# The last block of a fused attention and expert feed-forward kernel: z products by halves, one rounding remainder on GpSimd, another order on VectorE

## The reference, cut to what matters

```python
t = nx.reshape(-1, Dq)
probs = softmax(t @ gate_w.T); topw, topi = top_k(probs, 2); topw /= sum(topw)
h1 = t @ w1.T + 2.0 * (t @ a1[e].T) @ b1[e].T
h3 = t @ w3.T + 2.0 * (t @ a3[e].T) @ b3[e].T
act = silu(h1) * h3                                   # 512 wide, per expert
out_e = act @ w2.T + 2.0 * (act @ a2[e].T) @ b2[e].T  # 128 wide
out = sum_e weights[e] * out_e
x = x + out
```

## Time and profile before

| | us |
|---|---|
| median of three runs | 297.6 |
| span of the profiled execution | 296.7 |
| PE busy | 287.4 (97%) |
| DVE busy | 221.4 (75%) |
| ACT busy | 187.5 (63%) |
| POOL busy | 187.0 (63%) |

### The profile page before, as it was taken

How to read it: one execution, slowest core, us unless ns; L and a number is a source line. 1 busy time by engine, 2 the same in 40 slices (tenths; PEclk the granted TensorE clock), 3 DMA queues, 4 the chain that set the end, 5 groups by cost and what they waited for, 6 DMA issues and landing times. The chain is left out here.

```text
span 296.7 us, 4518 instructions
## 1 busy us (share of the span) xinstructions
PE 287.4 (97%) x1487; PEld 238.4 (80%) x1487; DVE 221.4 (75%) x607; ACT 187.5 (63%) x310; POOL 187.0 (63%) x186
## 2 busy tenths in 40 slices
PE   8779999999999999999999999999999999999995
PEld 6557888878888888888888888888888887878874
DVE  3878986995689658894589765895579965795295
ACT  1467967674945966757755868459656658655532
POOL 3375599288970889419990589608982389518930
PEclk9979999999999999999999999999999999999999
DMA  5720020200220021200211011200012000200002
GB/s 147 287 66 9 0 73 1 72 1 11 97 73 0 0 72 38 71 1 2 71 50 60 0 49 59 71 0 2 1 37 73 0 0 35 75 1 0 0 2 71
DMA packets 7225, 12.45 MB, mean 42 GB/s; under 512 B 1825, under 2 KB 3234, under 8 KB 7202
## 3 DMA queue, kind: packets, MB, share of 16 engines
q1 hardware_dynamic: 6768, 11.77, 12.0%
q10 hardware_dynamic: 434, 0.39, 0.4%
HBM read 10.03 MB, written 2.13 MB: 41 GB/s over the span
## 5 line engine op out<-in xcount | busy, mean ns | idle before, releaser
L989 ACT ACTIVATE silu<-h_ps 128x512 f32<-128x512 f32 x64 | 37.4, 596 | 31.4 <-PE h_ps L641 29.8
L1639 POOL TENSOR_TENSOR um_lo<-umf,um_hi 128x1024 fp32r<-128x1024 f32 x7 | 16.9, 2414 | 60.5 <-ACT um_hi L981 60.5
L641 PE MATMUL h_ps<-um_hi,b_hi 128*128 128x512 f32 x128 | 51.4, 401 | 0.0
L641 PE MATMUL h_ps<-um_lo,b_hi 128*128 128x512 f32 x128 | 50.3, 393 | 0.5 <-DVE um_lo L1309 0.5
L641 PE MATMUL h_ps<-um_hi,b_lo 128*128 128x512 f32 x128 | 49.9, 390 | 0.0
L1322 DVE TENSOR_TENSOR act_first<-silu,h_ps 128x512 f32<-128x512 f32 x32 | 21.4, 680 | 20.9 <-ACT silu L989 16.1
L1322 DVE TENSOR_TENSOR act_second<-silu,h_ps 128x512 f32<-128x512 f32 x32 | 21.7, 679 | 16.6 <-PE h_ps L641 14.7
L1661 POOL TENSOR_TENSOR scaled<-act_second,ratio 128x512 f32<-128x512 f32 x24 | 31.5, 1313 | 1.3 <-DVE act_second L1322 1.3
L641 PEld LDWEIGHTS h_ps<-um_lo,b_hi 128*128 128x128 f32 x128 | 24.0, 188 | 6.9 <-DVE um_lo L1309 1.4
L981 ACT CAST um_hi<-umf 128x1024 fp32r<-128x1024 f32 x14 | 14.8, 1055 | 23.2 <-DVE umf L1303 22.2
L641 PEld LDWEIGHTS h_ps<-um_hi,b_lo 128*128 128x128 f32 x128 | 24.1, 188 | 4.5
(11 more groups left out here) (278 smaller groups left out, 789.2 us busy)
## 6 DMA issues: line engine op xcount, KB each, us to landing
chosen<-choice_dram SPq DMA_DIRECT2D x7, 512.0 KB, 3.6
x_in<-in_x_dram SPq DMA_DIRECT2D x7, 256.0 KB, 2.9
ctx_in<-in_ctx_t_dram SPq DMA_DIRECT2D x7, 256.0 KB, 3.2
out_dram<-y SPq DMA_DIRECT2D x7, 256.0 KB, 2.0
act_second<-in_hidden_w_dram SPq DMA_DIRECT2D x1, 512.0 KB, 4.1
act_second<-in_lora_w_dram SPq DMA_DIRECT2D x1, 512.0 KB, 5.6
v_parts<-in_down_w_dram SPq DMA_DIRECT2D x1, 512.0 KB, 5.3
ctx_in<-in_ctx_t_dram ACTq DMA_DIRECT2D x2, 128.0 KB, 3.2
```

The lines of the kernel that those rows point to most:

```text
L641: mm = nc.tensor.matmul((h1_ps, h3_ps)[s][n % 2][:], b13[w][:, s, c * P:(c + 1) * P], um[k][m][:, s, :], start=False, stop=(i == 2), skip_ ...
L989: nc.scalar.activation(silu[:, n % SILU_RING, :], h1_ps[n % 2][:], ACT.Silu).then_inc(silu_done.sem, 1)
L1639: nc.gpsimd.tensor_tensor(um[1][1][:], umf[1][:], as_f32(um[1][0][:]), ALU.subtract)\
```

## The change: what it does

In the last block alone:

- `z_ps` is split by halves of two tiles: half 0 in `z_ps`, half 1 in `h3_ps[1]`, a bank that the hidden steps have left free; each half has its own completion count (`last_a2z_mm`). A 512-column matmul becomes two of 256 columns, all three terms of half 0 before those of half 1.
- the w2 products of the two halves, so far alternating, come apart: half 0 of all chunks first, then half 1, with `last_b2(0)` ahead of the last product of half 1.
- the lo part of chunk 3 of b moves from DVE to POOL (`last_b_low`), as POOL's last instruction.
- DVE does both `total`s and then both `z_low`s, then both halves of the b part of v, then `finish(LAST - 1)`, and then part, sum and lo part half by half.

```diff
-LAST_W2_ORDER = (1, 0, 3, 2)
+LAST_W2_FIRST = 1
+        last_z = (z_ps, h3_ps[1])
@@ a2_product
+                elif b == LAST and (c, k) == (3, 1):
+                    pe.wait_ge(last_b_lo, 1)
+                if b == LAST and k == 0:
+                    if c == first:
+                        pe.wait_ge(act_done.sem, act_done.of(LAST))
+                    for h in range(2):
+                        for i, (w, m) in enumerate(TERMS):
+                            mm = nc.tensor.matmul(last_z[h][:, 0:HALF], w2a2[w][:, c, D:D + ER],
+                                                  split[m][:, c, half(h)], start=(c == first and i == 0),
+                                                  stop=(c == last and i == 2), skip_group_check=True)
+                        if c == last:
+                            mm.then_inc(last_a2z_mm, 1)
+                    return
@@ PE, order of the last block
             a2_product(LAST, 0, 1)
-            w2_product(LAST, 1)
+            last_w2(1, 0)
             a2_product(LAST, 2, 1)
             a2_product(LAST, 0, 0)
+            a2_product(LAST, 1, 0)
             a2_product(LAST, 3, 1)
-            a2_product(LAST, 1, 0)
             a2_product(LAST, 2, 0)
             a2_product(LAST, 3, 0)
-            w2_product(LAST, 0)
-            w2_product(LAST, 3)
-            w2_product(LAST, 2)
+            last_w2(0, 0)
+            last_w2(2, 0)
+            last_w2(3, 0)
+            last_w2(1, 1)
+            last_w2(0, 1)
+            last_w2(2, 1)
             last_b2(0)
+            last_w2(3, 1)
             last_b2(1)
@@ POOL
+            def last_b_low():
+                pool.wait_ge(b_hi_done.sem, b_hi_done.of(LAST, 3))
+                nc.gpsimd.tensor_tensor(b_split[1][:, PARTS[2], :], act_second[:, PARTS[2], :],
+                                        as_f32(b_split[0][:, PARTS[2], :]), ALU.subtract).then_inc(last_b_lo, 1)
...
             scale_step(LAST, 2)
+            last_b_low()
```

More of the change, by code:

```diff
@@ L240, in build_program @@
         y_bank, out_bank = even_ps, odd_ps
-        last_out, last_turned = (odd_ps, h1_ps[0]), (even_ps, h3_ps[0])
+        last_out, last_turned, last_z = (odd_ps, h1_ps[0]), (even_ps, h3_ps[0]), (z_ps, h3_ps[1])
         choice_dram = nc.dram_tensor("choice_dram", (2, P * CHOICE), F32).ap()
@@ L361, in build_program @@
         stored = signal("stored", 16)
+        last_b_lo = sem("last_b_lo")
+        last_a2z_mm = sem("last_a2z_mm")
         last_v_part = [sem("last_v_part0"), sem("last_v_part1")]
@@ L691, in w2_product @@
                     pe.wait_ge(z_lo_done.sem, z_lo_done.of(b, c - 1))
-                first = (FIRST_W2_ORDER if b == 0 else LAST_W2_ORDER if b == LAST else W2_ORDER)[0]
+                first = (FIRST_W2_ORDER if b == 0 else W2_ORDER)[0]
                 if c == first:
-                    if b + 1 < BLOCKS:
-                        pe.wait_ge(t_hi_done.sem, t_hi_done.of(b + 1))
-                        pe.wait_ge(t_lo_done.sem, t_lo_done.of(b + 1))
-                    else:
-                        pe.wait_ge(o_t_done.sem, o_t_done.of(b - 1))
-                        pe.wait_ge(silu_done.sem, silu_done.of(b))
-                        pe.wait_ge(act_done.sem, act_done.of(b))
+                    pe.wait_ge(t_hi_done.sem, t_hi_done.of(b + 1))
+                    pe.wait_ge(t_lo_done.sem, t_lo_done.of(b + 1))
@@ new lines, in w2_product, with last_w2 @@
+                for i, (w, m) in enumerate(TERMS):
+                    nc.tensor.matmul(out_bank[:], w2a2[w][:, c, 0:D], z_split[m][:, c, :],
+                                     start=(c == first and i == 0), stop=False, skip_group_check=True)
+            def last_w2(c, h):
+                if c < 2:
+                    pe.wait_ge(z_lo_pair.sem, z_lo_pair.of(LAST))
+                else:
+                    pe.wait_ge(z_lo_done.sem, z_lo_done.of(LAST, c - 1))
+                if c == LAST_W2_FIRST:
+                    if h == 0:
+                        pe.wait_ge(o_t_done.sem, o_t_done.of(LAST - 1))
+                    else:
+                        pe.wait_ge(silu_done.sem, silu_done.of(LAST))
+                        pe.wait_ge(act_done.sem, act_done.of(LAST))
@@ L701, in w2_product @@
                 for i, (w, m) in enumerate(TERMS):
[L702 to L708, removed]
+                    nc.tensor.matmul(last_out[h][:, 0:HALF], w2a2[w][:, c, 0:D], z_split[m][:, c, half(h)],
+                                     start=(c == LAST_W2_FIRST and i == 0), stop=False, skip_group_check=True)
@@ L1390, in last_part @@
             def last_part(k, i):
-                done = (a2z_mm, a2b_mm)[k]
-                ve.wait_ge(done.sem, done.of(LAST))
                 if k == 1:
+                    ve.wait_ge(a2b_mm.sem, a2b_mm.of(LAST))
                     ve.wait_ge(mask_scaled.sem, mask_scaled.of(LAST))
+                else:
+                    ve.wait_ge(last_a2z_mm, i + 1)
                 ve.wait_ge(v_done.sem, v_done.of(LAST - 1))
-                nc.vector.scalar_tensor_tensor(out=v_parts[:, k, half(i)], in0=(z_ps, b_ps)[k][:, half(i)],
+                src = last_z[i][:, 0:HALF] if k == 0 else b_ps[:, half(i)]
+                nc.vector.scalar_tensor_tensor(out=v_parts[:, k, half(i)], in0=src,
                                                scalar=LORA_SCALE, in1=masks[LAST % 2][:, k, half(i)],
@@ L1558, in _ @@
             total(LAST, 2)
-            b_low(LAST, 2)
             total(LAST, 3)
             z_low(LAST, 1)
+            z_low(LAST, 2)
             last_part(1, 0)
-            z_low(LAST, 2)
+            last_part(1, 1)
             finish(LAST - 1)
             last_part(0, 0)
+            last_sum(0)
             last_part(0, 1)
-            last_sum(0)
-            last_part(1, 1)
+            last_low(0)
             last_sum(1)
-            last_low(0)
             last_low(1)
```

## The result

The changed kernel takes 299.79 us (median of 10 runs, 298.72 to 300.02) against 298.38 for the kernel before in the same comparison (10 runs). The ratio is 1.0045, 95% interval 1.003 to 1.0059: 1.3 us slower by the ratio (the medians lie 1.41 apart), inside the forecast's "no change, near its edge". The profiled execution has a span of 298.2 against 296.7. Two executions, one of e9 (736.43) and one of the kernel before (891.33), took more than twice the usual time and are left out of every ratio.

What follows compares the result with a forecast made beforehand. The prediction took PE and DVE as full in the last block, DVE having to come free earlier too. +1.10 - 0.60 + 0.34 + 0.18 = +1.02, plus 0.25, is +1.27: span about 298.0, time 298.9 us, range 297.4 to 299.9.

Steps and rivals of the forecast that it cites:

- no change, near its edge: Whole kernel: forecast 0.4% slower, within the about 0.5% (1.5 us) that a measurement can't tell from no change; chance 0.73.
- Two engines full, both late at once: Last block, 284.5 to 288.0: PE and DVE busy 3.50 of 3.50 us, ending together at 289.29 and 289.31.
- POOL's b_lo blocks DVE's total, +1.10: Last block: POOL's b_lo gets in behind DVE's scaled, so DVE's first total ends at 286.63, +1.10 us.
- the starved case: Rival: DVE keeps winning, POOL's b_lo ends only at 288.69 and PE waits; 300.0 us, 0.8% slower; chance 0.12.
- the shared one: Rival: beside POOL each two-operand DVE instruction takes 0.3 longer, two totals +0.60; 298.4 us; chance 0.10.
- no blocking: Rival: POOL's b_lo and DVE's totals don't block each other in any way worth naming; 297.8 us; chance 0.15.
- -0.60, +0.34, +0.18 to the z part: DVE ahead of v's z part: one b_lo less -0.60, second b part moved ahead +0.34, ACT waits +0.18.
- New order of v, +0.25: Last block, from v's z part to the second b2 product: 3.24 us in place of 2.99, +0.25.
- The halves hidden: PE's z in halves: half 0 done 0.36 us before half 1, but the gain is hidden behind DVE.
- The sum, +1.27: Whole kernel: +1.02 to the z part and +0.25 behind it, span 296.7 to about 298.0, time 298.9 us.

Runs made afterwards that it cites:

- e9: e8 with one of the two w2 products ahead of b's last chunk (half 1's) put back behind z's; ratio 0.9982 to the kernel before.
- e6: Changed kernel with b_lo on DVE and DVE's order of before, leaving only the halves on PE; ratio 1.0006 to the kernel before.
- e4: Kernel before plus one idle 128x512 POOL subtraction where the change puts b_lo, nobody waiting for it; ratio 1.0029 to the kernel before.
- e1: Changed kernel with the lo part of b's chunk 3 back on DVE, between the two totals; ratio 1.0010 to the kernel before.
- e3: Changed kernel with both sums of v ahead of both lo parts; ratio 1.0013 to the kernel before.
- e11: e8 run once more, unchanged, to narrow its interval; ratio 0.9987 to the kernel before.
- e8: e7 with y of the block before moved behind v's lo parts, last transpose and residual given another bank and tile; ratio 0.9986 to the kernel before.
- e2: Kernel before with only the lo part of b's chunk 3 moved from DVE to POOL; ratio 1.0039 to the kernel before.
- e7: Changed kernel with b_lo on DVE behind both totals, v's sums ahead of its lo parts, PE's w2 products reordered; ratio 0.9999 to the kernel before.
- e10: Kernel before plus one idle 1024-column POOL copy, SBUF to SBUF, at the place of e4's subtraction; one run, no ratio, last residual at 10.75 against 9.91.
- e5: Kernel before plus four idle POOL memsets at the place of e4's subtraction; one run, no ratio, last residual at 9.91 as before.

## Why the prediction was right, point by point

- **Two engines full, both late at once.** Nearly right. DVE was not quite the last: e6 shows that z done earlier starts the z part 0.09 earlier with DVE unchanged. I had read y's end from its row, 288.19 + 1.12 = 289.31; but the next instruction can start 0.08 before that (after the change y starts at 289.56 and the z part at 290.59, 1.03 later). So PE's z, not y, set 289.33, by 0.1.
- **POOL's b_lo blocks DVE's total, +1.10.** Right: +1.11 (1.59 before and 2.70 now, from the start of scaled to the end of the first total), and e4 has it alone, +1.12. POOL got in ahead of a DVE instruction that was next in line, which no row before had shown; the starved case did not come, nor the shared one (e4), nor no blocking. By the time alone this could not be told: the starved case was put at 300.0, nearer to the 299.79 than the forecast's 298.9. The trace decides it: b_lo is done at 286.44, and what PE waits for is z_lo, not b_lo.
- **-0.60, +0.34, +0.18 to the z part.** The z part was worked out at +1.02; it is +0.91. The missing 0.1 is the point above: the change takes away the small wait for PE. e1, with the terms +0.34 and ACT's waits alone, gives +0.41 (0.50 by the same working, 0.40 without the same 0.1).
- **New order of v, +0.25.** Right sign, too large: from the z part to the second b2 product 3.15 against 2.99 (290.59 to 293.74), +0.16. I had put 0.10 before each dependent DVE instruction; part to sum takes 0.04 here (291.00 to 291.04). e3 shows that the order is a loss: 0.24 of it comes back at the second b2 product.
- **The halves hidden.** Right: e6.
- **The sum, +1.27.** +1.07 in the last block. The forecast time of 298.9 came from the three runs known then, median 297.6. The median over the comparison is 298.38, and with its own base the forecast would be 299.65, against 299.79. So the waits were the right ones and their sizes right to 0.1 each (0.2 too large together), while the time lies only 0.1 inside the upper end of the stated range (297.4 to 299.9), because the base was 0.78 too low: that it lies inside is in part luck.

What is left between +1.07 in the block and +1.34 by the ratio is not seen in the code that changed. The executions of every version fall into two groups by the mean granted clock of the whole span, 0.996 to 1.000 or 0.994 and below, with medians for the kernel before, over the three comparisons with e1 to e11, of 297.44 (35 runs) and 298.67 (51 runs). Of the changed kernel's ten runs nine were in the lower group, median 299.82: +1.15 within that group. Its one run in the higher group has 298.72, +1.28. That the change makes the lower group more frequent was not shown: e8 and e11 are one kernel and had 10 and 11 of 12 in it, and e9, which has one product elsewhere in the last block, 6 of 11.

Within the lower group alone the medians follow the traces. Each version against the kernel before of its own comparison, with the trace's last residual in brackets: e4 +1.08 (+1.12), e3 +0.62 (+0.76), e2 +0.58 (+0.68), e1 +0.48 (+0.58), e6 -0.03 (+0.06), e7 -0.16 (-0.10), e8 -0.86 (-0.68), e11 -0.75 (-0.68), e9 -0.75 (-0.65). The ratios in the table mix the two groups, so they blur differences that are there.

## What to carry to other kernels

An idle engine is not a free one: before a two-operand VectorE instruction goes to GpSimd, look at what VectorE does in that stretch. Here it was full of instructions with two operands in SBUF, and GpSimd's one cost it 1.12 us, nearly GpSimd's whole 1.30, where doing the work itself costs VectorE 0.60. In the trace this was one long busy instruction (1.78 for 0.68) and no idle time, so compare the ends of instructions on both engines before believing a busy share. And put work that nobody waits for (here y of the block before) where its engine waits for another anyway: from e7 to e8 that was worth 0.58 us in the trace, where the halves alone (e6) were worth nothing.

## What the runs showed of the hardware

**DVE and POOL.** The Trainium skill (SBUF — State Buffer, section Who interferes with whom) says that a DVE instruction with two SBUF inputs contends with a GpSimd instruction that reads SBUF and not with one that only writes it. e4, e10 and e5 agree: 1.78 and 1.52 against 0.68. The same section lets issue order decide who blocks, and the trace agrees: in every handover read here the one already waiting went first, even ahead of an instruction that DVE would have started back to back (POOL's b_lo has its start at 284.92, DVE's total at 285.21). It has no number for the handover. Here a 512-column DVE instruction ends 0.54 to 0.55 after POOL's, a 512-column POOL instruction with two inputs 1.15 after DVE's, 0.13 to 0.15 less than each takes alone.

**TensorE's clock at the start.** I had not expected that most of the 1.2 us between the two groups comes from one place, far from the change. Windows of the kernel before, profiled at a mean clock of 0.992 (the third number from the end is the granted clock):

```profile
10.00:20.00 10.00, 7.52 (x35) 5.56 (x34) 7.46 (x32) 5.41 (x11) 6.43 (x10) 0.83 0.33 120
```

The same of e7, profiled at 0.999:

```profile
10.00:20.00 10.00, 6.48 (x35) 4.40 (x34) 8.29 (x37) 6.11 (x13) 7.02 (x12) 1.00 0.37 133
```

In the first, a part of this stretch, from about 16 to 19 us, runs at the lower of the two levels, 1.2 GHz in place of 2.4. Ahead of that PE waits three times in block 0, for ACT, for a transfer and for POOL: 0.62, 0.45 and 1.35 us up to 12.0, 13.1 and 15.6. In the second all of it is at 2.4, though PE waits nearly as long there (0.62, 0.67, 1.14). Why it falls in some executions and not in others is open. The trace of e4, whose code up to POOL's last instruction is that of the kernel before, shows what it costs: PE's products with `wo_sb` take 0.68 in place of 1.20 and 1.06, and it is ahead of the other trace by 0.27 at 15.3, by 1.25 at 17.4 and by 1.10 at DVE's last scaled. DVE's last scaled starts at 283.8 to 284.3 where this stretch has 0.71 to 0.84, and at 282.8 to 283.0 where it has 1.00, in all thirteen traces, whatever the version. So in this kernel a difference below 1 us is read from places within one trace, not from two spans.
